# An attention on one Trainium2 core: softmax sums taken by the exponentials, a loop written out, and adds in another order

## The chip, the cores and the metric

The kernel runs on one core of a Trainium2 chip. The metric is the time of one execution on the device in microseconds, lower is better.

## The reference, cut to what is computed

The program is four transformer layers on x of 8 sequences by 100 tokens by 512 features, with a second input `ctx` of 8 by 361 by 512. Each layer adds a cross-attention to `ctx` and a feed-forward block, both behind a layer norm:

```python
x = x + _L0_xattn_ref(_layernorm(x), ctx, ids, ...)
x = x + _L0_ffn_ref(_layernorm(x), ...)
x = x + _L1_xattn_ref(_layernorm(x), ctx, mask, ...)
x = x + _L1_ffn_ref(_layernorm(x), ...)
x = x + _L2_xattn_ref(_layernorm(x), ctx, ...)
x = x + _L2_ffn_ref(_layernorm(x), ...)
x = x + _L3_xattn_ref(_layernorm(x), ctx, ctx, mask, ...)
x = x + _L3_ffn_ref(_layernorm(x), ...)
```

Layer 2's attention, the one whose arithmetic the change touches (16 heads of 32):

```python
Q, K, V = query @ Wq.T + bq, key_value @ Wk.T + bk, key_value @ Wv.T + bv
scores = einsum('bhsd,bhtd->bhst', Q, K) / sqrt(32)
ctx = einsum('bhst,bhtd->bhsd', softmax(scores, axis=-1), V)
return ctx @ Wo.T + bo
```

Layer 1's is the same with the scores clipped to [-50, 50], a mask and a norm on its result. Layer 0's has its keys and values behind a latent, a window of ids as its mask, and 16 heads of 128, so that its output is a product with a weight of 2048 by 512: `out @ W_o`, which is added to x.

## The kernel before

Each engine (PE, ACT, DVE, POOL, and SP for transfers) has its own stream of instructions; they are ordered among each other by semaphores alone. `engine.wait_ge(s, n)` (or `wait`, L94, which leaves out a wait for nothing) holds that engine and all that is queued behind it there. x stays on the chip, features in the partitions, in four blocks of 128 by 800 tokens. Every large product is made of three: values are split into a high and a low part, and `product` (L101) issues high by high (L106), low operand by high (L107) and high by low (L109).

**The two attentions of one class.** `Attention` (layer 2, l2x) and its subclass `BoundedAttention` (layer 1, l1x) go over the 8 sequences, here called contexts. `batches` (L1647) sets how: context 0 in full, contexts 1 to 4 as a loop of two turns with two contexts each, contexts 5 to 7 in full. All five engines' streams are made by it. A context has 4 units m of 4 heads each; unit number i is 4 b + m. In one step PE's queue is (`pe_batch`):

- S, the scores of the next unit (L2158, three products of 4 heads, into the banks 0 to 3). It waits for k_lo of that unit.
- O, the output of the unit before (`pe_output`, L2141): twelve matmuls with a matrix of ones, which put the sum of a row's exponentials into 32 partitions for each head (bank 6), and twelve with the values v.
- the keys of the next context for block m (L106, L107, L109).
- T, twelve transposes of the unit's exponentials (L2124), into the columns 0:400 of the banks 4 to 6. They wait for the exponentials and for `o`, since O's results lie in the same banks, columns 400:500.
- V, the values of the next context (not in step 3).

ACT's queue in a step (`act_batch`): the four exponentials of the next unit (L2165; they wait for DVE's shift), xn_hi of the output (L2203, waits for `o`), k_hi (L1863), at m = 2 the queries of the next context, the copy of T's first two tiles (`turned_01`, L2196), and at m = 1 the high part of the context after next (L1817), for which POOL makes the low part (L1809). DVE's queue (`dve_batch`): maxima of the next unit in two pairs (L2208), each followed by the shift made from it (L2212), the reciprocal of the sums (L2247, 128x100 out of PSUM) and the multiplication with it (L2252, `o`), k_lo (L1869), the copy of T's third tile (`turned_2`, L2235), xn_lo (L2257), and the add of the values' bias (L1875).

**Layer 0's output loop** (l0x) goes over 8 pairs of heads, j; turns 0, 1, 6 and 7 are written out, 2 to 5 are a loop. Before the last turn PE makes in each the fused weight of the next pair (`pe_fuse_output`, 1.4 us), and then four units of twelve products, unit m into the bank pair m % 2; unit m waits for the add of unit m - 2, which frees the banks. ACT takes the high part of the fused weight (L3650) and of the heads' output (L3589), and of three slabs of weights that SP loads (L3645), of which POOL makes the low parts (L3270). DVE makes the low part of the fused weight (L3861), two low parts of the output (L3866) and the four adds into x (L3756), in that order.

## Time and profile before

| | |
|---|---|
| time, median of 3 runs | 2216.07 us (2214.10 to 2216.55) |
| time of the profiled execution | 2215.22 us |
| its span | 2213.3 us |
| busy: PE, DVE, ACT, POOL | 92%, 48%, 41%, 23% |
| mean granted clock of PE | 0.969 |
| layer 0's attention, its feed-forward block | 0 to 497, to 694 us |
| layer 1's | to 965, to 1085 us |
| layer 2's | to about 1385, to 1610 us |
| layer 3's | to 1890, to 2213 us |

Times in the profile are microseconds from the start of the span. PE is the engine of matmuls, PEld its loading of weights, L12 is line 12 of the kernel. In a row of a timeline the square bracket tells how long the engine stood before the instruction and which instruction ended that; "issue" is time in which it waited for nothing that the profile shows. A row may join several like instructions (x4).

### The profile page before, as it was taken

The numbers are of one execution on the slowest core, as the hardware profiler recorded it, in microseconds if no ns is written. First come the engines' busy times: TensorE is split into PE (matmuls) and PEld (weight loads), VectorE is DVE, ScalarE is ACT, GpSimd is POOL, SyncE is SP. The second block draws the span as 40 slices with busy tenths as digits, with TensorE's granted clock in tenths as the row PEclk, the third lists the DMA queues.
The fourth block names the chain that finished last, engine by engine and source line by source line (L and its number), as shares of the span: only waits on it lengthen the run. The fifth ranks groups of instructions, "written<-read, shape, count | busy, mean of one in ns | idle before, by whom it ended". The sixth has DMA issues, their size and how long they took to land.

```text
span 2213.3 us, 39269 instructions
## 1 busy us (share of the span) xinstructions
PE 2034.3 (92%) x14719; PEld 1645.7 (74%) x14719; DVE 1061.3 (48%) x2393; ACT 908.1 (41%) x1740; POOL 501.4 (23%) x358
## 2 busy tenths in 40 slices
PE   7989999887997999977899999999989999799996
PEld 6977776775446877764687777999989999655554
DVE  5556666663114465688646666323244555311111
ACT  3346666432224454576645454422253222222221
POOL 3333332312343211000221010233241110023232
PEclk9999999998998999988999999999999999899998
DMA  3200000228444211131110000222220000589995
GB/s 121 85 14 28 27 28 20 67 99 292 77 84 140 76 67 67 40 153 42 47 47 15 28 14 2 82 63 61 66 75 24 28 27 1 190 281 324 318 323 141
DMA packets 91367, 203.91 MB, mean 92 GB/s; under 512 B 9194, under 2 KB 14414, under 8 KB 89070
## 3 DMA queue, kind: packets, MB, share of 16 engines
q1 hardware_dynamic: 79790, 175.06, 23.8%
q0 software_dynamic: 11424, 26.75, 5.8%
q8 instruction: 104, 1.70, 0.3%
q14 instruction: 49, 0.40, 0.1%
HBM read 184.08 MB, written 21.43 MB: 93 GB/s over the span
## 4 chain that ended last, share of the span: by engine, by line
PE 68%; DMA 12%; DVE 9%; ACT 5%; issue 4%; SPq 1%; POOL 1%; DVEq 0%; ACTq 0%; POOLq 0%
PE psum L106 15%; PE psum L109 14%; PE psum L107 14%; DMA l3f_sum_dram<-l3f_y,l3f_rows 9%; PE psum L900 3%; PE psum L3516 3%; PE psum L3484 2%; PE psum L2710 2%; PE psum L3502 2%; PE psum L2124 2%; PE psum L926 1%; PE psum L2353 1%; PE psum L2725 1%; DVE l2x_highest L2208 1%; PE psum L2938 1%
## 5 line engine op out<-in xcount | busy, mean ns | idle before, releaser
L1534 PE MATMUL psum<-l3f_gate_up,l3f_x_turned 128*128 128x352 f32 x496 | 154.0, 464 | 0.8 <-ACT l3f_x_turned L1593 0.8
L1534 PEld LDWEIGHTS psum<-l3f_gate_up,l3f_x_turned 128*128 128x128 f32 x496 | 92.9, 192 | 48.0 <-issue 1.7
L2165 ACT ACTIVATE l2x_probs<-psum,l2x_shift 100x361 f32<-100x361 f32 x128 | 64.9, 559 | 99.7 <-DVE l2x_shift L2212 98.3
L1809 POOL TENSOR_TENSOR l2x_ctx_lo<-l2x_ctx_raw,l2x_ctx_hi 128x1448 fp32r<-128x1448 f32 x8 | 26.3, 3294 | 330.5 <-ACT l2x_ctx_hi L1817 330.5
L3655 ACT ACTIVATE l0x_probs<-l0x_probs,l0x_lowest 100x361 f32<-100x361 f32 x128 | 75.2, 588 | 42.3 <-DVE l0x_lowest L3819 42.2
L106 PE MATMUL psum<-xn_hi,l2f_w_gu_hi 128*128 128x400 f32 x256 | 88.6, 346 | 1.6 <-DVE xn_lo L192 1.3
L1509 POOL DMA_INDIRECT l3f_sum_dram<-l3f_y,l3f_rows x31 | 49.2, 1586 | 180.3 <-DMA l3f_sum_dram<-l3f_y,l3f_rows 151.7
L1619 DVE TENSOR_TENSOR l3f_h<-l3f_silu,psum 128x352 f32<-128x352 f32 x31 | 16.2, 521 | 151.7 <-ACT l3f_silu L1606 138.3
L107 PE MATMUL psum<-xn_lo,l2f_w_gu_hi 128*128 128x400 f32 x256 | 87.9, 343 | 0.0
L1560 PE MATMUL psum<-l3f_down,l3f_h_turned 128*128 128x512 f32 x186 | 85.1, 593 | 0.9 <-DVE l3f_h_turned L1625 0.9
L2382 ACT ACTIVATE ln_squares<-l1x_clipped,l1x_key_shift,l1x_key_scale 128x400 f32<-128x400 f32 (+1 forms) x96 | 62.3, 712 | 53.3 <-DVE l1x_clipped L2421 53.3
L448 POOL TENSOR_TENSOR l2f_w_gu_lo<-l2f_raw_gu,l2f_w_gu_hi 128x512 fp32r<-128x512 f32 x32 | 43.0, 1356 | 180.9 <-ACT l2f_w_gu_hi L463 180.9
L3819 DVE CUSTOM_DVE_ANT_0 l0x_probs<-psum,l0x_outside 100x361 f32<-100x361 f32 x128 | 62.9, 531 | 32.4 <-PE psum L3484 29.5
L900 PE MATMUL psum<-l0f_weights,l0f_x_turned 128*128 x160 | 74.0, 606 | 1.2 <-ACT l0f_x_turned L1042 0.8
L3516 PE MATMUL psum<-ln_squares,l0x_l_turned 128*128 128x400 f32 (+1 forms) x192 | 73.0, 516 | 0.0
L647 DVE TENSOR_TENSOR l2f_h<-l2f_silu,psum 128x800 f32<-128x800 f32 x16 | 15.8, 988 | 119.1 <-PE psum L109 119.1
L2744 ACT ACTIVATE ln_squares<-psum 64x64 f32<-64x64 f32 x128 | 27.9, 218 | 105.9 <-PE psum L2710 103.5
L1606 ACT ACTIVATE l3f_silu<-psum 128x352 f32<-128x352 f32 x31 | 14.4, 464 | 138.2 <-PE psum L1534 138.2
L109 PE MATMUL psum<-xn_hi,l2f_w_gu_lo 128*128 128x400 f32 x256 | 68.6, 344 | 0.0
L1809 POOL TENSOR_TENSOR l1x_ctx_lo<-l1x_ctx_raw,l1x_ctx_hi 128x1448 fp32r<-128x1448 f32 x8 | 26.5, 3310 | 139.7 <-ACT l1x_ctx_hi L1817 139.7
L2208 DVE TENSOR_REDUCE l2x_highest<-psum 100x2 f32<-100x722 f32 x64 | 57.9, 905 | 0.1
L139 PE MATMUL psum<-identity,residual 128*100 128x128 f32 x248 | 42.0, 340 | 16.5 <-DVE xn_lo L192 5.8
(534 smaller groups left out, 6108.0 us busy)
## 6 DMA issues: line engine op xcount, KB each, us to landing
l3f_gate_up<-in_slabs_dram SPq DMA_DIRECT2D x31, 1280.0 KB, 7.7
l3f_down<-in_slabs_dram SPq DMA_DIRECT2D x31, 512.0 KB
l0x_w_raw<-in_slabs_dram SPq DMA_DIRECT2D x52, 256.0 KB, 2.7
l0f_weights<-in_slabs_dram SPq DMA_DIRECT2D x8, 1536.0 KB
l1x_piece<-in_bit_w_dram SPq DMA_DIRECT2D x8, 1024.0 KB, 6.8
l1f_raw<-in_bit_w_dram SPq DMA_DIRECT2D x8, 1024.0 KB, 9.1
l2f_raw_gu<-in_slabs_dram SPq DMA_DIRECT2D x32, 256.0 KB, 2.6
l3f_down<-in_slabs_dram SPq DMA_DIRECT2D x31, 192.0 KB
```

Of the source, the lines that this page charges most:

```text
L106: pe.matmul(outs[i], weight_hi, moving[i][0], start=first, stop=False)
L107: pe.matmul(outs[i], weight_hi, moving[i][1], start=False, stop=False)
L109: mm = pe.matmul(outs[i], weight_lo, moving[i][0], start=False, stop=last)
L900: mm = pe.matmul(c.psum[:, t % 2, :], self.x_turned[:, t % 2, k, :], self.weights[:, bass.DynSlice(expert, 1), k * 512:(k + 1) * 512].rear ...
L1534: mm = pe.matmul(c.psum[:, bank + x, 0:self.INNER], self.x_turned[:, t % 2, k, :], self.gate_up[:, q, at:at + self.INNER], start=k == 0, s ...
L1560: mm = pe.matmul(c.psum[:, 6 + t % 2, :], self.h_turned[0:z - a, t % 2, k, :], self.down[0:z - a, q, k, :], start=k == 0, stop=k == 2)
L2165: act.activation(self.probs[:, m % 2, g, :], c.psum[0:S, g, 0:C], ACT.Exp, bias=self.shift[:, g:g + 1], scale=self.SCALE).then_inc(self.s( ...
L2208: dve.tensor_reduce(self.highest[:, heads], c.psum[0:S, heads, 0:C], AX.X, ALU.max).then_inc(self.s("maxima"), 1)
L2382: act.activation(self.exps(c, m)[0:z - a, t, :], self.clipped[0:z - a, t, :], ACT.Exp, bias=shift, scale=scale).then_inc(self.s("exps"), 1)
L3516: mm = pe.matmul(c.psum[:, 6, 0:4 * S], self.l_turned[0:z - a, q, t, :], turned[0:z - a, t, :], start=t == 0, stop=t == 2)
L3655: act.activation(self.probs[:, g, :], self.probs[:, g, :], ACT.Exp, bias=self.lowest[:, g:g + 1], scale=-1.0, accum_out=self.total[:, g:g ...
L3819: dve.tensor_tensor_reduce(self.probs[:, g, :], c.psum[0:S, g, 0:C], self.outside[:, q, :], -self.SCALE, 3.0e38, ALU.add, ALU.min, self.lo ...
```

## The change

Three parts.

1. In `Attention`, and so in layer 2 alone: the exponentials also give their sums (`accum_out`, one number for each row and head). DVE turns them into inverses (100x4) and copies each into 32 columns (`by_row`, 100x128); PE transposes that to 128x100 in bank 6, columns 400:500; DVE copies it into SBUF (`spread`), and the multiplication reads it there. The twelve ones-matmuls of each unit and the reciprocal of 128x100 are gone. The transpose stands at the head of PE's step, ahead of the scores, and waits for `by_row` and for `turned_2` of the unit before, whose source lies in the same bank. `BoundedAttention` has methods of its own for its sums; those are not touched.
2. In `BoundedAttention`, layer 1, `batches` writes all 8 contexts out, on all engines; there is no loop.
3. In layer 0's output loop DVE's order is L3861, add 0, low output 0, add 1, low output 1, adds 2 and 3.

```diff
@@ -1644,8 +1644,12 @@
 KEY_TILES = [(0, P), (P, 2 * P), (2 * P, C)]
 
 
-def batches(engine, body):
-
+def batches(engine, body, in_full=False):
+
+    if in_full:
+        for b in range(B):
+            body(b, b % 2, b + 1 < B, b + 2 < B)
+        return
     turns = (B - 4) // 2
     body(0, 0, True, True)
     with engine.Fori(0, turns) as i:
@@ -1666,6 +1670,7 @@
     VALUES_BANK = 7
     EARLY_UNITS = (7,)
     V_SHAPE = [P, 2, 3, D]
+    IN_FULL = False
     SCALE = 1.0 / float(HD) ** 0.5
 
     def __init__(self, name, index, slabs_at):
@@ -1698,7 +1703,9 @@
         self.probs = c.sb(own, n + "_probs", [S, 2, GROUP, C])
         self.highest = c.sb(own, n + "_highest", [S, GROUP])
         self.shift = c.sb(own, n + "_shift", [S, GROUP])
-        self.inverse = c.sb(own, n + "_inverse", [P, S])
+        self.total, self.inverse = (c.sb(own, n + x, [S, 2, GROUP]) for x in ("_total", "_inverse"))
+        self.by_row = c.sb(own, n + "_by_row", [S, 2, P])
+        self.spread = c.sb(own, n + "_spread", [P, S])
         self.o = c.sb(own, n + "_o", [P, 2, S])
 
     def turned(self, c):
...
@@ -1956,6 +1963,7 @@
         self.pe_scores(c, pe, 0, 0, 0)
 
     def pe_after_batches(self, c, pe):
+        self.pe_inverse(c, pe, B * KD - 1, KD - 1)
         self.pe_output(c, pe, B - 1, (B - 1) % 2, KD - 1)
 
     def pe_outputs_ready(self, pe):
...
@@ -2071,6 +2079,7 @@
         self.dve_project(c, dve)
 
     def dve_last_output(self, c, dve):
+        self.dve_spread(c, dve, B * KD - 1)
         self.dve_output(c, dve, B - 1, KD - 1)
         self.dve_output_low(c, dve, B - 1, KD - 1)
 
@@ -2100,6 +2109,8 @@
 
         for m in range(KD):
             i = b * 4 + m
+            if m or not isinstance(b, int) or b:
+                self.pe_inverse(c, pe, i - 1, m + 1)
             if m < 3:
                 self.pe_scores(c, pe, b, q, m + 1)
             elif more:
@@ -2127,6 +2138,13 @@
             if more and m < 3:
                 self.pe_values(pe, b + 1, 1 - q, m)
 
+    def pe_inverse(self, c, pe, i, m):
+
+        pe.wait_ge(self.s("by_row"), i + 1)
+        pe.wait_ge(self.s("turned_2"), i + 1)
+        pe.transpose(c.psum[:, 6, 400:400 + S], self.by_row[:, m % 2, :], c.identity[0:S, 0:S]).then_inc(
+            self.s("inverse_units"), 1)
+
     def pe_output(self, c, pe, b, q, m):
 
         i, turned = b * 4 + m, self.turned(c)
@@ -2134,15 +2152,11 @@
         pe.wait_ge(self.s("turned_2"), i + 1)
         if m == 0:
             pe.wait_ge(self.s("v_added"), b * 3 + 3)
-        for x in range(2):
-            for t, (a, z) in enumerate(KEY_TILES):
-                for g in range(GROUP):
-                    head = slice((m * GROUP + g) * HD, (m * GROUP + g + 1) * HD)
-                    mm = pe.matmul(c.psum[g * HD:(g + 1) * HD, 4 + m % 2 if x else 6, 400:400 + S],
-                                   self.v[0:z - a, q, t, head] if x else c.ones[0:z - a, 0:HD],
-                                   turned[0:z - a, t, g * S:(g + 1) * S], start=t == 0, stop=t == 2)
-            if x == 0:
-                mm.then_inc(self.s("total_units"), 1)
+        for t, (a, z) in enumerate(KEY_TILES):
+            for g in range(GROUP):
+                head = slice((m * GROUP + g) * HD, (m * GROUP + g + 1) * HD)
+                mm = pe.matmul(c.psum[g * HD:(g + 1) * HD, 4 + m % 2, 400:400 + S], self.v[0:z - a, q, t, head],
+                               turned[0:z - a, t, g * S:(g + 1) * S], start=t == 0, stop=t == 2)
         mm.then_inc(self.s("pv_units"), 1)
 
     def pe_scores(self, c, pe, b, q, m):
@@ -2163,7 +2177,7 @@
         wait(act, self.s("t_units"), i - 1)
         for g in heads:
             act.activation(self.probs[:, m % 2, g, :], c.psum[0:S, g, 0:C], ACT.Exp, bias=self.shift[:, g:g + 1],
-                           scale=self.SCALE).then_inc(self.s("exps"), 1)
+                           scale=self.SCALE, accum_out=self.total[:, m % 2, g:g + 1]).then_inc(self.s("exps"), 1)
 
     def act_before_batches(self, c, act):
         self.act_exps(c, act, 0, 0, range(0, 2))
@@ -2173,7 +2187,17 @@
         self.dve_maxima(c, dve, 0, 0)
         self.dve_maxima(c, dve, 0, 1)
         self.dve_values(dve, 0, 0, 1)
+        self.dve_inverse(dve, 0, 0)
         self.dve_values(dve, 0, 0, 2)
+
+    def dve_inverse(self, dve, i, m):
+        dve.wait_ge(self.s("exps"), (i + 1) * GROUP)
+        dve.reciprocal(self.inverse[:, m % 2, :], self.total[:, m % 2, :]).then_inc(self.s("inverses"), 1)
+        dve.wait_ge(self.s("inverses"), i + 1)
+        wait(dve, self.s("inverse_units"), i - 1)
+        dve.tensor_copy(self.by_row[:, m % 2, :].rearrange("p (g e) -> p g e", g=GROUP),
+                        self.inverse[:, m % 2, :].unsqueeze(2).broadcast_to([S, GROUP, HD])).then_inc(
+                            self.s("by_row"), 1)
 
     def act_batch(self, c, act, b, q, more, two_more):
         turned = self.turned(c)
@@ -2216,6 +2240,8 @@
         turned = self.turned(c)
         for m in range(KD):
             i = b * 4 + m
+            if m or not isinstance(b, int) or b:
+                self.dve_spread(c, dve, i - 1)
             if m < 3 or more:
                 self.dve_maxima(c, dve, i + 1, 0)
                 self.dve_maxima(c, dve, i + 1, 1)
@@ -2237,19 +2263,23 @@
                 self.dve_output_low(c, dve, b, m - 1)
             elif not isinstance(b, int) or b:
                 self.dve_output_low(c, dve, b - 1, KD - 1)
+            if m < 3 or more:
+                self.dve_inverse(dve, i + 1, m + 1)
             if more and m < 3:
                 self.dve_values(dve, b + 1, 1 - q, m)
 
+    def dve_spread(self, c, dve, i):
+        dve.wait_ge(self.s("inverse_units"), i + 1)
+        wait(dve, self.s("o"), i)
+        dve.tensor_copy(self.spread[:, :], c.psum[:, 6, 400:400 + S]).then_inc(self.s("spread"), 1)
+
     def dve_output(self, c, dve, b, m):
         i = b * 4 + m
-        dve.wait_ge(self.s("total_units"), i + 1)
-        wait(dve, self.s("o"), i)
-        dve.reciprocal(self.inverse[:, :], c.psum[:, 6, 400:400 + S]).then_inc(self.s("inverses"), 1)
-        dve.wait_ge(self.s("inverses"), i + 1)
+        dve.wait_ge(self.s("spread"), i + 1)
         dve.wait_ge(self.s("pv_units"), i + 1)
         wait(dve, self.s("o_hi"), i - 1)
         wait(dve, self.s("o_lo"), i - 1)
-        dve.tensor_tensor(self.o[:, m % 2, :], c.psum[:, 4 + m % 2, 400:400 + S], self.inverse[:, :], ALU.mult).then_inc(
+        dve.tensor_tensor(self.o[:, m % 2, :], c.psum[:, 4 + m % 2, 400:400 + S], self.spread[:, :], ALU.mult).then_inc(
             self.s("o"), 1)
 
     def dve_output_low(self, c, dve, b, m):
@@ -2264,6 +2294,7 @@
 
 class BoundedAttention(Attention):
     BOUND = 50.0
+    IN_FULL = True
     EPS = 1e-8
     SCALE_MAX = 0.3
 
@@ -3738,23 +3769,24 @@
         self.dve_normalise(c, dve, 0)
         batches(dve, lambda b, q, more, two_more: self.dve_batch(c, dve, b, q, more))
 
-        def split_output(j, q):
-            self.low_fused(c, dve, j, q)
-            for x in range(2):
-                self.low_output(c, dve, j, q, x)
+        def added(j, m):
+            dve.wait_ge(self.s("out_units"), j * 4 + m + 1)
+            if not isinstance(j, int) or j:
+                dve.wait_ge(self.s("added"), j * 4 + m - 3)
+            into = c.residual[:, m, :].rearrange("p (h t) -> p h t", h=2)
+            dve.tensor_tensor(into, into, c.psum[:, 2 * (m % 2):2 * (m % 2) + 2, 0:HALF], ALU.add).then_inc(
+                self.s("added"), 1)
 
         def out(j, q, more):
-            if more:
-                split_output(j + 1, 1 - q)
             if not more:
                 return tail_dve(dve, c.norms[self.index + 1], last_added)
-            for m in range(KD):
-                dve.wait_ge(self.s("out_units"), j * 4 + m + 1)
-                if not isinstance(j, int) or j:
-                    dve.wait_ge(self.s("added"), j * 4 + m - 3)
-                into = c.residual[:, m, :].rearrange("p (h t) -> p h t", h=2)
-                dve.tensor_tensor(into, into, c.psum[:, 2 * (m % 2):2 * (m % 2) + 2, 0:HALF], ALU.add).then_inc(
-                    self.s("added"), 1)
+            self.low_fused(c, dve, j + 1, 1 - q)
+            added(j, 0)
+            self.low_output(c, dve, j + 1, 1 - q, 0)
+            added(j, 1)
+            self.low_output(c, dve, j + 1, 1 - q, 1)
+            added(j, 2)
+            added(j, 3)
 
         def last_added(h, m):
             j, u = self.PAIRS - 1, h * KD + m
```

The hunks left out pass `self.IN_FULL` to `batches` in the other engines' streams.

## Rows read from the trace of the kernel before

**Rows 1.** Busy us by stretch (windows): layer 2's attention; columns PE, PEld, DVE, ACT, POOL.
```profile
1137.00:1385.00 248.00, 231.09 (x2912) 187.84 (x2911) 157.74 (x310) 125.11 (x234) 24.89 (x10) 1.00 0.06 18
```

**Rows 2.** Waits of the stretch 391 to 497 us: total, times, longest.
```profile
PE psum L106 <- DVE residual L3756: 9.7, 8, 1.3
```

**Rows 3.** Timeline of layer 0's output loop: start, duration, engine, line.
```profile
408.18 1.02 ACT L3650 ACTIVATE l0x_out_w_hi<-psum 128x1024 fp32r<-128x1024 f32 x1 [7.81 <-PE psum L109]
...
410.37 2.44 DVE L3866 TENSOR_TENSOR l0x_o_lo<-l0x_q_latent,l0x_o_hi 128x800 fp32r<-128x800 f32 x2
...
412.73 1.87 DVE L3756 TENSOR_TENSOR residual<-residual,psum 128x800 f32<-128x800 f32 x2
...
413.76 0.45 PE L106 MATMUL psum<-l0x_o_hi,l0x_out_w_hi 128*128 128x400 f32 x1 [1.33 <-DVE residual L3756]
...
419.83 1.03 ACT L3650 ACTIVATE l0x_out_w_hi<-psum 128x1024 fp32r<-128x1024 f32 x1 [7.76 <-PE psum L109]
```

**Rows 4.** Busy us by stretch (windows): two contexts of layer 1; PEclk stands near the end.
```profile
777.30:805.40 28.10, 26.90 (x424) 22.32 (x428) 18.01 (x40) 14.74 (x25) 3.33 (x1) 1.00 0.21 65
805.40:838.60 33.20, 28.48 (x426) 23.66 (x428) 18.09 (x41) 14.38 (x24) 3.32 (x1) 0.95 0.16 57
```

**Rows 5.** Timeline of PE at layer 1's back edge.
```profile
830.69 0.43 PE L106 MATMUL psum<-l1x_ctx_hi,l1x_w_hi 128*128 128x362 f32 x1 [4.33 <-issue]
```

**Rows 6.** Waits of the stretch 1137 to 1385 us, the longest of kind issue.
```profile
PEld psum L2124 <- issue: 4.7, 9, 1.3
```

**Rows 7.** Timeline of one step of layer 2's attention.
```profile
1240.43 0.42 PE L2158 MATMUL psum<-l2x_k_hi,l2x_qh_hi 32*100 32x362 f32 x4
...
1241.11 0.72 PE L2141 MATMUL psum<-ln_squares,ones 128*32 128x100 f32 x24
...
1241.65 0.70 PE L2141 MATMUL psum<-ln_squares,l2x_v 128*32 128x100 f32 x24
...
1242.48 2.12 ACT L2165 ACTIVATE l2x_probs<-psum,l2x_shift 100x361 f32<-100x361 f32 x4 [4.17 <-DVE l2x_shift L2212]
...
1243.48 0.78 DVE L2247 RECIPROCAL l2x_inverse<-psum 128x100 f32<-128x100 f32 x1
...
1245.09 1.27 PE L2124 MATMUL psum<-identity,l2x_probs 100*128 100x100 f32 x12 [0.55 <-DVE l2x_o L2252]
1245.16 0.55 ACT L1863 ACTIVATE l2x_k_hi<-psum,l2x_vectors 128x362 fp32r<-128x362 f32 x1
1245.74 0.59 DVE L1869 SCALAR_TENSOR_TENSOR l2x_k_lo<-psum,l2x_vectors,l2x_k_hi 128x362 fp32r<-128x362 f32 x1 [0.90 <-ACT l2x_k_hi L1863]
...
1249.37 0.41 PE L2158 MATMUL psum<-l2x_k_hi,l2x_qh_hi 32*100 32x362 f32 x4
```

**Rows 8.** Timeline at the turn of a context in layer 2.
```profile
1258.63 0.41 PE L2158 MATMUL psum<-l2x_k_hi,l2x_qh_hi 32*100 32x362 f32 x4
...
1263.66 0.59 DVE L1869 SCALAR_TENSOR_TENSOR l2x_k_lo<-psum,l2x_vectors,l2x_k_hi 128x362 fp32r<-128x362 f32 x1 [0.90 <-ACT l2x_k_hi L1863]
...
1264.21 0.41 PE L2158 MATMUL psum<-l2x_k_hi,l2x_qh_hi 32*100 32x362 f32 x4
...
1264.32 0.58 DVE L2235 COPY ln_squares<-psum 105x400 f32<-105x400 f32 x1
```

**Rows 9.** Timelines of layer 2: POOL's splits of two contexts, and DVE beside the first.
```profile
1248.61 3.31 POOL L1809 TENSOR_TENSOR l2x_ctx_lo<-l2x_ctx_raw,l2x_ctx_hi 128x1448 fp32r<-128x1448 f32 x1 [29.36 <-ACT l2x_ctx_hi L1817]
1281.00 3.29 POOL L1809 TENSOR_TENSOR l2x_ctx_lo<-l2x_ctx_raw,l2x_ctx_hi 128x1448 fp32r<-128x1448 f32 x1 [29.09 <-ACT l2x_ctx_hi L1817]
...
1251.21 0.73 DVE L2212 TENSOR_SCALAR l2x_shift<-l2x_highest 100x2 f32<-100x2 f32 x1
```

**Rows 10.** Timeline of ACT in layer 0: exponentials with accumulation.
```profile
216.19 0.60 ACT L3655 ACTIVATE l0x_probs<-l0x_probs,l0x_lowest 100x361 f32<-100x361 f32 x1 [1.05 <-DVE l0x_lowest L3819]
216.69 0.19 ACT L3655 ACTIVATION_READ_ACCUMULATOR l0x_probs<-l0x_probs,l0x_lowest 100x1 f32 x1
216.78 0.58 ACT L3655 ACTIVATE l0x_probs<-l0x_probs,l0x_lowest 100x361 f32<-100x361 f32 x1
```

More of the change, by code:

```diff
@@ L1765, in body @@
                     self.slab(c, sp, i)
-        batches(sp, body)
+        batches(sp, body, self.IN_FULL)
     def sync_more(self, c, sp):
@@ L1799, in body @@
                     self.split_weight(pool, i)
-        batches(pool, body)
+        batches(pool, body, self.IN_FULL)
     def split_output_weights(self, act, b, m):
@@ L1915, in pe @@
         self.pe_start(c, pe)
-        batches(pe, lambda b, q, more, two_more: self.pe_batch(c, pe, b, q, more))
+        batches(pe, lambda b, q, more, two_more: self.pe_batch(c, pe, b, q, more), self.IN_FULL)
         self.pe_after_batches(c, pe)
@@ L2023, in act @@
         self.act_before_batches(c, act)
-        batches(act, lambda b, q, more, two_more: self.act_batch(c, act, b, q, more, two_more))
+        batches(act, lambda b, q, more, two_more: self.act_batch(c, act, b, q, more, two_more), self.IN_FULL)
         self.act_finish(c, act)
@@ L2061, in dve @@
         self.dve_before_batches(c, dve)
-        batches(dve, lambda b, q, more, two_more: self.dve_batch(c, dve, b, q, more))
+        batches(dve, lambda b, q, more, two_more: self.dve_batch(c, dve, b, q, more), self.IN_FULL)
         self.dve_finish(c, dve)
```

## The prediction, made before the changed kernel was run

> **What bounds the kernel now.** The busy windows come first: in layer 2's attention PE is busy 231 of 248 us at the full clock [rows 1]. That speaks for less work on PE, but PE waits in most steps too, so each stretch is read from its waits and its timeline.
>
> Layer 0's output loop: among the waits PE stands 9.7 us, in 8 places, for an add of L3756 [rows 2]. In the timeline of an iteration (11.65 us, from one L3650 to the next) DVE has its queue in this order: L3861, two L3866 (2.44 us), then the add that frees the bank, ending 0.93 us after its start at 412.73. PE's third unit waits for it 1.33 us, to 413.76 [rows 3].
>
> Layer 1: one context takes 28.1 us, the one that holds the loop's back edge 33.2 [rows 4]. There PE stands 4.33 us, for nothing that the profile shows ("issue") [rows 5].
>
> Layer 2: the longest such wait is 1.3 us [rows 6], so no back edge costs anything like that. The timeline of a step [rows 7] shows a ring. S (scores) at 1240.43; DVE takes maxima; ACT starts four exponentials at S+2.05 (2.12 us); then k_hi and DVE's k_lo, to 1246.33; PE's values V start 0.06 later and the next S follows them. PE is not the ring's slow part: it runs out of work before T (transposes), where it waits 0.55 us for o (L2252), and V stands behind T's 1.27 us in PE's queue. At the turn of a context there is no V: S starts at 1264.21, right at the end of T, 5.58 us after the S before [rows 8].
>
> **Layer 0's adds.** No instruction is new; add 0 goes ahead of both L3866 and add 1 between them. Add 0 then follows L3861's end at 410.46 and ends about 411.45; PE wants it at 412.3. L3866, add 1: 412.7, 413.7, and PE wants that one at 414.5. The second L3866 and adds 2 and 3 end at about 417.7, still before the next fused product's L3861 needs DVE. PE's wait goes: four units of 12 products at 0.18 us (8.8) and the fusion's 6 (1.4) leave 10.15 us an iteration, 1.5 less; seven iterations give -10.5. What is late next is ACT's L3650, which waits for PE alone, then POOL's split and SP's slabs, whose slack of over 1 us in the period stays. Bounds: -7 (1 us each) to -11.
>
> **Layer 1 in full.** Same instructions, on all five engines (SP's context loads and POOL's split too), no branch. The stall's price is 33.2 less 28.1: -5.1. Bounds: 0, if it is code that comes late however it is laid out, and -5.1.
>
> **Layer 2.** Removed on PE: 12 ones-matmuls a unit, 0.54 us between the first of the ones group and the first of the values group [rows 7]; added: one transpose, 0.1 us (a twelfth of T's 1.27). Over 32 units that is -14 us of PE work. On DVE the reciprocal of 0.78 us goes; a reciprocal and a copy of 100 rows (0.17 us each, as L2212 [rows 9], the nearest of that size) and the spread (a quarter us, as the multiplication of L2252) come. Both removals lie between S and T, where PE stands for exponentials and o anyhow. So I follow the ring:
> - S to first exponential. DVE's v-add (0.69 us) ends at S+0.79, and the maxima follow at once; the spread now goes between them: 2.05+0.24.
> - Exponentials. An accumulating one is followed by a read of 0.19 us, and the next starts 0.09 us after that read [rows 10]: 0.59 apart instead of 0.52, and 0.1 behind the last. I take +0.31 a unit. From below it is 0; from above 0.75, four whole reads.
> - First exponential to k_hi: 2.68 in the row, held by o; o is now early, and 2.12+0.31 with xn_hi's 0.2 and gaps is 2.70. k_hi to the end of k_lo 1.17, to V 0.06, V to S 2.98, and the new transpose ahead of S 0.10.
> The sum is 9.30 instead of 8.94 us. The steps that were longer than that already (9.26, where DVE's shift took 0.73 us beside POOL's split [rows 9]) gain nothing and lose nothing: 9.30.
> - The turn. The new transpose waits for turned_2 of the unit before and stands ahead of S on PE. turned_2 (0.58 us, L2235) is queued on DVE behind k_lo. S+2.29+2.70+1.17 gives k_lo's end at 6.16, turned_2 at 6.79, transpose, S at 6.96, where it was 5.58. Behind it wait S, the maxima and all the ring.
> A context went 32.4 us (from the two splits [rows 9]); it goes 9.30x3+6.96 = 34.86, +2.4. Seven contexts with a successor: +16.8. The last output loses reciprocal and ones (1.3) from the tail and pays slower exponentials (0.4): -0.9. Together +16. Bounds: with reads and spread at nothing only the turn's share and the transpose are left, +8; with serial reads (0.44 more a unit, 14) some +25 after what other waits cover.
>
> **Sum.** -10.5-5.1+16 = +0.4. On the profiled execution's 2215.22 us that is 2215.6; the median of the three runs lies 0.85 above that execution, so **2216.5**. A change under 0.2%, 4.4 us, is about what a measurement of this kernel can't tell from none.
>
> **The pages.** The Trainium skill, "Runtime: NRT & Kernel Launch", section "Instruction fetch mechanics", says that a taken branch to a target outside the current two pages of instructions forces a fetch before execution goes on. Layer 1's stall agrees with that; layer 2's loop, where no row shows one, doesn't. By the page the whole 5.1 us go, and a DVE or ACT loop that grows could get such a stall of its own.
>
> **Rivals.**
> 1. PE's work counts (0.08). PE is busy 93% of the stretch [rows 1], and if the o wait (0.55) and the ones are what sets the step, layer 2 gives -14, and the whole is 2215.2-10.5-5.1-14+0.85 = 2186.5. Against it: S to T is filled by exponentials in the row; V waits for k_lo.
> 2. Cheap accumulation (0.20). The reads overlap and the spread slips in: layer 2 +8, 2208.5. For it: ACT's reads overlap the next exponential by half already [rows 10].
> 3. **Slower**: DVE's new small copy, by_row, meets POOL's split of 3.31 us (0.25). The shift of 0.17 us took 0.73 there [rows 9]. In the new step by_row comes 7.3 to 7.5 us after S (turned_2's end at 6.8, output_low 0.25, reciprocal 0.17), and POOL's split at 7.8, where the rows have 8.2: T needs no o any more and ends half a microsecond earlier [rows 7, 9]. They miss each other by 0.3 us. If it falls in and is held by about 1.7 us, six splits give +10: 2226.5. It decides when ACT's L1817 ends earlier than by_row starts. Serial reads (+9) end in the same place. For a held copy speaks the Trainium skill, "SBUF — State Buffer", section "SBUF: two separate sides": VectorE and GpSimd share a pair of ports as an exclusive lock. The row of L2212 agrees with it in part: it waited about 0.56 us, not for all of the split.
> 4. Layer 1's stall stays, or moves into another stretch (0.07): 2221.6.
> 5. PE's clock: the context with the 4.33 us of standing shows a mean granted clock of 0.95 of the full 2.4 GHz, where the one before shows 1.00 [rows 4]; a turn with some 1.9 us of standing in place of 0.3 might do so too. After the 1.33 us in the output loop it did not [rows 3]. I give this no chance of its own; its price, some tenths of a microsecond per turn, is inside the upper bound.
> That a part does nothing at all (DVE's order hidden in layer 0) would need that PE waits there for another; the waits name only the add [rows 2].
>
> **How the numbers follow.** Forecast 0.40, at 2216.5, its own range 2212 to 2221. Rivals 1 and 2 are faster, 0.28, and a little of the forecast's own lower side: faster 0.31. Rivals 3 and 4 are slower, 0.32, less what of them stays within 4.4 us: slower 0.29. Same 0.40. The range leaves out rival 1 and the ends of rivals 2 and 3: 2204 to 2227.
>
> **What would show it.** Layer 0: iteration of 10.15 us, no wait for L3756 on PE. Layer 1: all splits of contexts 28.1 us apart. Layer 2: PE's new transpose waits for L2235 about 1.3 us at each turn; V steps at 9.3; splits 34.9 apart; reads of about 0.19 us behind each L2165. The forecast is wrong if the splits there stay near 32 us apart (rival 2, or 1 below that), or if by_row's copy takes over half a microsecond (rival 3).

## The result, and where the time went

The changed kernel takes 2203.3 us (median of 5 runs, 2202.33 to 2206.84); the kernel before took 2216.55 on the same chip (5 runs). The ratio is 0.9944, with a 95% interval from 0.9930 to 0.9959. It is faster by some 12 us. The forecast was no change, at 2216.5, and the measured time lies just under its range of 2204 to 2227.

The page of the changed kernel (first part):

```profile
span 2201.5 us, 37754 instructions
...
PE 2013.6 (91%) x13983; PEld 1630.8 (74%) x13983; DVE 1047.7 (48%) x2457; ACT 911.4 (41%) x1868; POOL 504.4 (23%) x358
```

PE has 736 matmuls fewer and is busy for 20.7 us less, yet its share of the span fell only from 92% to 91%. Lined up with the trace before, by the start of like instructions on POOL and ACT, the time moves thus:

| stretch | forecast | profiled executions |
|---|---|---|
| layer 0's output loop | -10.5 | -10.4 |
| layer 0's feed-forward block | 0 | +2.3 |
| layer 1's attention | -5.1 | -6.1 |
| layer 2's attention | +16 | +3.1 |
| everything else | 0 | -0.7 |
| span | +0.4 | -11.8 |

The +3.1 us of layer 2 is too low by 1.7 us: the profiled execution of the kernel before had a stretch of low clock (0.53, 1384.00 to 1387.50) behind its last scores. From there to the feed-forward block it took 30.9 us, where e1, e2, e4 and e6, in which this code is as before, took 29.2; the changed kernel took 27.2.

**Layer 0.** The timeline of ACT in the output loop, the rows that answer to [rows 3] (L3681 was L3650):

```profile
396.55 1.02 ACT L3681 ACTIVATE l0x_out_w_hi<-psum 128x1024 fp32r<-128x1024 f32 x1 [1.83 <-PE psum L109]
...
416.69 1.03 ACT L3681 ACTIVATE l0x_out_w_hi<-psum 128x1024 fp32r<-128x1024 f32 x1 [6.16 <-PE psum L109]
...
457.21 1.02 ACT L3681 ACTIVATE l0x_out_w_hi<-psum 128x1024 fp32r<-128x1024 f32 x1 [6.29 <-PE psum L109]
```

From 396.55 to 457.21 are six iterations, 10.11 us each, where the forecast had 10.15 and the kernel before 11.65. Of the eight waits of PE for an add one is left, 1.2 us in the last turn.

**Layer 1.** The timeline of POOL, the split of each context (L1816 was L1809):

```profile
774.52 3.32 POOL L1816 TENSOR_TENSOR l1x_ctx_lo<-l1x_ctx_raw,l1x_ctx_hi 128x1448 fp32r<-128x1448 f32 x1 [8.16 <-ACT l1x_ctx_hi L1824]
802.45 3.31 POOL L1816 TENSOR_TENSOR l1x_ctx_lo<-l1x_ctx_raw,l1x_ctx_hi 128x1448 fp32r<-128x1448 f32 x1 [24.61 <-ACT l1x_ctx_hi L1824]
830.34 3.32 POOL L1816 TENSOR_TENSOR l1x_ctx_lo<-l1x_ctx_raw,l1x_ctx_hi 128x1448 fp32r<-128x1448 f32 x1 [24.58 <-ACT l1x_ctx_hi L1824]
```

They are 27.93 and 27.89 us apart. The context with the stall ([rows 4], 33.2 us) is like the others, and all of them are 0.2 us shorter than the 28.1 of before.

**Layer 2.** The waits of PE, 1120 to 1376 us (total, times, longest):

```profile
PE psum L106 <- DVE l2x_k_lo L1876: 15.9, 21, 1.2
PE psum L2145 <- DVE ln_squares L2261: 12.5, 11, 1.4
PE psum L2135 <- ACT l2x_probs L2179: 1.7, 3, 0.8
```

Two of them are new or nearly so: V waits for k_lo in all 21 steps that have values (before, 1.4 us in 3 of them), and the new transpose (L2145) waits 12.5 us for turned_2 (L2261). Now one step with values, to set beside [rows 7]. New lines: L2172 scores, L1882 v-add, L2274 spread, L2232 maxima, L2179 exponentials, L2227 xn_hi, L1870 k_hi, L1876 k_lo:

```profile
1237.21 0.41 PE L2172 MATMUL psum<-l2x_k_hi,l2x_qh_hi 32*100 32x362 f32 x4
1237.23 0.69 DVE L1882 TENSOR_TENSOR l2x_v<-psum,l2x_bv 128x512 f32<-128x512 f32 x1 [2.14 <-PE psum L109]
...
1237.84 0.25 DVE L2274 COPY l2x_spread<-psum 128x100 f32<-128x100 f32 x1
...
1238.01 0.91 DVE L2232 TENSOR_REDUCE l2x_highest<-psum 100x2 f32<-100x722 f32 x1
...
1239.24 0.56 ACT L2179 ACTIVATE l2x_probs<-psum,l2x_shift 100x361 f32<-100x361 f32 x1 [3.65 <-DVE l2x_shift L2236]
...
1239.70 0.19 ACT L2179 ACTIVATION_READ_ACCUMULATOR l2x_probs<-psum,l2x_shift 100x1 f32 x1
1239.80 0.55 ACT L2179 ACTIVATE l2x_probs<-psum,l2x_shift 100x361 f32<-100x361 f32 x1
...
1241.44 0.28 ACT L2227 ACTIVATE xn_hi<-l2x_o 128x100 f32 x1
1241.61 0.56 ACT L1870 ACTIVATE l2x_k_hi<-psum,l2x_vectors 128x362 fp32r<-128x362 f32 x1
...
1242.21 0.59 DVE L1876 SCALAR_TENSOR_TENSOR l2x_k_lo<-psum,l2x_vectors,l2x_k_hi 128x362 fp32r<-128x362 f32 x1 [1.60 <-ACT l2x_k_hi L1870]
...
1242.86 0.48 PE L106 MATMUL psum<-l2x_w_hi,l2x_ctx_hi 128*105 128x512 f32 x1 [0.73 <-DVE l2x_k_lo L1876]
...
1245.95 0.42 PE L2172 MATMUL psum<-l2x_k_hi,l2x_qh_hi 32*100 32x362 f32 x4
```

S to S is 8.74 us; the forecast had 9.30, the row before 8.94. Two prices of the forecast are not paid here.

The first is the spread, which takes 0.17 us from its start to that of the maxima. The v-add starts 0.02 us after S, where before it was 0.10, since the transpose now stands between V and S: that makes 0.08 us of room. The rest was there before. The maxima wait for the scores as well as for the v-add; in the trace of the kernel before they start at S+0.80 at the turns too (1265.01, with S at 1264.21), where no v-add stands ahead of them. So they still start at S+0.80, and the exponentials at S+2.03.

The second is the reads of the sums. First exponential to xn_hi is 2.20 us (1239.24 to 1241.44), and the kernel before had 2.21 in the loop where `o` held it least (1251.97 to 1254.18 in its trace). But there ACT stood twice within that time, for the second shift and 0.09 us for `o`. The reads now fill these stands; what they cost where there are none, e4 shows.

The turn of a context, to set beside [rows 8]:

```profile
1250.95 0.59 DVE L1876 SCALAR_TENSOR_TENSOR l2x_k_lo<-psum,l2x_vectors,l2x_k_hi 128x362 fp32r<-128x362 f32 x1 [1.60 <-ACT l2x_k_hi L1870]
1251.46 0.56 DVE L2261 COPY ln_squares<-psum 105x400 f32<-105x400 f32 x1
...
1252.17 0.28 PE L2145 MATMUL psum<-identity,l2x_by_row 100*128 100x100 f32 x1 [1.30 <-DVE ln_squares L2261]
...
1252.38 0.55 PE L2172 MATMUL psum<-l2x_k_hi,l2x_qh_hi 32*100 32x362 f32 x4
...
1252.72 0.52 PE L2172 MATMUL psum<-l2x_k_lo,l2x_qh_hi 32*100 32x362 f32 x4
...
1253.58 0.91 DVE L2232 TENSOR_REDUCE l2x_highest<-psum 100x2 f32<-100x722 f32 x1 [0.74 <-PE psum L2172]
...
1254.84 0.56 ACT L2179 ACTIVATE l2x_probs<-psum,l2x_shift 100x361 f32<-100x361 f32 x1 [3.09 <-DVE l2x_shift L2236]
```

The mechanism is the forecast's: turned_2 behind k_lo, then the transpose, then S, at 6.43 us after the S before (1245.95) in place of 5.58; the forecast had 6.96. What the forecast gave no chance of its own came too: after the stand of 1.30 us the scores' products take 0.52 us instead of 0.33. The granted clock beside it, for the three microseconds after this turn and after another with the same stand:

```profile
1252.30:1255.30 3.00, 3.00 (x39) 2.18 (x39) 2.07 (x5) 0.47 (x2) 0.00 (x0) 0.53 0.00 0
1219.70:1222.70 3.00, 3.00 (x47) 2.54 (x47) 2.32 (x5) 0.89 (x3) 0.00 (x0) 1.00 0.00 0
```

The number behind the five engines' is the granted clock: 0.53 here, near the lower of the two levels, and 1.00 at the other turn. It fell behind two of the seven turns, in e5's trace behind the same two. Here it cost 0.7 us (the step after this turn is 9.43 instead of 8.72). Behind the last turn, where PE goes from the scores to T without a stand, it cost 1.5 us: the step is 7.35 instead of 5.83. One product in that step, one in the next, and the clock (0.50) of the first:

```profile
1351.53 0.54 PE L107 MATMUL psum<-xn_lo,l2x_w_hi 128*128 128x400 f32 x1
...
1358.88 0.35 PE L107 MATMUL psum<-xn_lo,l2x_w_hi 128*128 128x400 f32 x1
...
1351.50:1354.50 3.00, 3.00 (x10) 2.98 (x10) 1.52 (x5) 2.46 (x9) 0.00 (x0) 0.50 0.01 3
```

Between the scores of units 1 and 31 the four traces of kernels with the transpose ahead of the scores (changed, e3, e5, e11) have two or three such falls each. The ten others, in which the scores of a turn start without a stand, have none. That ties the falls to this order, but not each to its turn: one in e3 (at 1160.11) and one in e11 (at 1159.15) began in a step with values, and cost 1.6 and 1.7 us.

### The profile page after: what moved, and what is told of

It reads as the page before. It is cut to its first block, busy times and chain, and to the rows that moved or that the text cites. A ratio compares the mean times of both kernels' runs of the same rounds, so it can differ in the third digit from the quotient of the medians.

```text
span 2201.5 us, 37754 instructions
## 1 busy us (share of the span) xinstructions
PE 2013.6 (91%) x13983; PEld 1630.8 (74%) x13983; DVE 1047.7 (48%) x2457; ACT 911.4 (41%) x1868; POOL 504.4 (23%) x358
## 4 chain that ended last, share of the span: by engine, by line
PE 66%; DMA 12%; DVE 9%; ACT 7%; issue 4%; SPq 1%; POOL 1%; DVEq 0%; ACTq 0%; POOLq 0%
PE psum L106 15%; PE psum L109 14%; PE psum L107 14%; DMA l3f_sum_dram<-l3f_y,l3f_rows 9%; PE psum L900 3%; PE psum L3547 3%; PE psum L3515 2%; PE psum L2741 2%; ACT l2x_probs L2179 2%; PE psum L3533 2%; PE psum L926 1%; PE psum L2384 1%; PE psum L2756 1%; PE psum L2969 1%; DVE l2x_highest L2232 1%
## 5 line engine op out<-in xcount | busy, mean ns | idle before, releaser
L2179 ACT ACTIVATE l2x_probs<-psum,l2x_shift 100x361 f32<-100x361 f32 x128 | 70.4, 559 | 122.0 <-DVE l2x_shift L2236 122.0
L1816 POOL TENSOR_TENSOR l2x_ctx_lo<-l2x_ctx_raw,l2x_ctx_hi 128x1448 fp32r<-128x1448 f32 x8 | 26.4, 3300 | 332.1 <-ACT l2x_ctx_hi L1824 332.1
L106 PE MATMUL psum<-xn_hi,l2f_w_gu_hi 128*128 128x400 f32 x256 | 88.6, 346 | 1.6 <-DVE xn_lo L192 1.3
L2775 ACT ACTIVATE ln_squares<-psum 64x64 f32<-64x64 f32 x128 | 27.9, 218 | 105.8 <-PE psum L2741 103.4
L2232 DVE TENSOR_REDUCE l2x_highest<-psum 100x2 f32<-100x722 f32 x64 | 57.9, 905 | 3.4 <-PE psum L2172 3.1
L1816 POOL TENSOR_TENSOR l1x_ctx_lo<-l1x_ctx_raw,l1x_ctx_hi 128x1448 fp32r<-128x1448 f32 x8 | 26.4, 3306 | 134.7 <-ACT l1x_ctx_hi L1824 134.7
L1816 POOL TENSOR_TENSOR l3x_ctx_lo<-l3x_ctx_raw,l3x_ctx_hi 128x1448 fp32r<-128x1448 f32 x8 | 26.3, 3289 | 131.9 <-ACT l3x_ctx_hi L1824 131.9
```

What stands on the lines that cost most here:

```text
L106: pe.matmul(outs[i], weight_hi, moving[i][0], start=first, stop=False)
L1816: pool.tensor_tensor(self.ctx_lo[:, q, :, :], self.ctx_raw[:, :, :], self.ctx_hi[:, q, :, :], ALU.subtract).then_inc(self.s("ctx_split"), 1)
L2179: act.activation(self.probs[:, m % 2, g, :], c.psum[0:S, g, 0:C], ACT.Exp, bias=self.shift[:, g:g + 1], scale=self.SCALE, accum_out=self.t ...
L2232: dve.tensor_reduce(self.highest[:, heads], c.psum[0:S, heads, 0:C], AX.X, ALU.max).then_inc(self.s("maxima"), 1)
```

## Experiments

Each was measured in turn with the kernel before on its chip; e1 to e4, e5 to e8 and e9 to e12 had one chip each, so between these groups ratios are compared. "Layer 2" is the time from the scores of unit 1 to those of unit 31 in the trace, 235.6 us in the kernel before.

| run | median us | ratio to before | 95% interval | layer 2, us |
|---|---|---|---|---|
| changed kernel | 2203.30 | 0.9944 | 0.9930 to 0.9959 | 242.3 |
| e1, adds only | 2207.00 | 0.9955 | 0.9940 to 0.9970 | |
| e2, layer 1 only | 2212.70 | 0.9978 | 0.9967 to 0.9989 | |
| e3, layer 2 only | 2222.70 | 1.0028 | 1.0017 to 1.0039 | 243.6 |
| e4, sums alone | 2217.67 | 1.0003 | 0.9993 to 1.0012 | 236.3 |
| e5, changed again | 2206.19 | 0.9953 | 0.9940 to 0.9966 | 242.4 |
| e6, without layer 2's part | 2200.06 | 0.9922 | 0.9909 to 0.9935 | 235.0 |
| e7, transpose behind the scores | 2196.90 | 0.9914 | 0.9902 to 0.9927 | 231.9 |
| e8, e7 and layer 2 written out | 2191.93 | 0.9892 | 0.9878 to 0.9906 | 228.6 |
| e9, old sums, layers 1 and 2 written out | 2195.52 | 0.9904 | 0.9883 to 0.9924 | 231.0 |
| e10, e8 with ones for nothing | 2199.02 | 0.9919 | 0.9899 to 0.9939 | 233.4 |
| e11, changed, spread twice | 2208.74 | 0.9962 | 0.9949 to 0.9975 | 247.0 |
| e12, e8, low part and inverses later | 2191.49 | 0.9887 | 0.9865 to 0.9909 | 225.8 |

**e1: which part does what, the adds.** Its edit is the last hunk of the diff alone.

> The kernel before with layer 0's adds moved, nothing else. Theory: PE's wait for the add was the whole of the loss, so an iteration of the output loop takes 10.1 us instead of 11.65 and the loop's end comes 10.4 us earlier; in the trace of the changed kernel 2.3 us of that were gone again at the end of the feed-forward block behind it (its last product waits for transfers of rows by index). If that loss belongs to the earlier start, this run is 8 us faster, about 2208.4, ratio 0.9963. Rival: the 2.3 us were chance of that one execution, and the run is 10.4 us faster, 2206.1, ratio 0.9953.

Measured 0.9955, some 10 us; the interval (6.7 to 13.3 us) holds both 8 and 10.4, so the time doesn't tell them apart. The traces do. From the last product of the output loop to the last of the feed-forward block, in which PE waits for rows that POOL moves by index, the fourteen traces of this study have between 200.2 and 204.2 us. Both ends are kernels whose layer 0 is as before (the kernel before and e4); the ten with the adds moved have 200.4 to 202.1, and the 202.1 is the changed kernel's. Its +2.3 us is within what these transfers differ by from one execution to the next. The theory as I had put it falls; the adds are worth their 10 us.

**e2: layer 1.**

```diff
 class BoundedAttention(Attention):
     BOUND = 50.0
+    IN_FULL = True
```

> The kernel before with layer 1's contexts written out, nothing else. Theory: the stall of 4.33 us at the back edge and the slow clock behind it go (5.1 us), and each of the four contexts that were in the loop runs 0.2 us shorter (27.9 instead of 28.1 in the trace of the changed kernel): 6.0 us faster, 2210.5, ratio 0.9973. Rival: the stall was not the loop's, and comes up elsewhere: ratio 1.000.

0.9978 is 4.9 us, with 2.4 to 7.3 in the interval, and from the second to the last of its eight splits the trace is 6.1 us shorter (173.8 instead of 179.9). The stall was the loop's.

**e3: layer 2 alone.** All of the first part of the change; layer 1 has its loop again, and the adds are as before.

> The kernel before with the new sums of layer 2, nothing else. Theory, by the trace of the changed kernel: steps with values 8.7 us where they were 8.7 to 9.2, turns 6.43 where they were 5.58, and slower steps without keys; +3.4 us in all, 2220, ratio 1.0015. The forecast's +16 would be 2232.5, ratio 1.0072. Rival: removed matmuls and reciprocal do pay here, and the loss in the changed kernel came with the other parts: ratio 0.999 or below.

It is slower by 6.2 us (3.8 to 8.6): the sign of the forecast and less than half of its size. This trace also shows the third rival at work, though not where the forecast saw it. In context 0 POOL splits weights (L1784), and DVE's small instructions from SBUF to SBUF run into it, by_row as well as the shift. The same pair in the changed kernel, POOL first, then DVE; and the two rows that the rival was about, where by_row passes the context's split by 0.6 us:

```profile
1139.49 1.29 POOL L1784 TENSOR_TENSOR l2x_w_lo<-l2x_out_raw,l2x_w_hi 128x512 fp32r<-128x512 f32 x1
1145.50 1.30 POOL L1784 TENSOR_TENSOR l2x_w_lo<-l2x_out_raw,l2x_w_hi 128x512 fp32r<-128x512 f32 x1 [4.72 <-ACT l2x_w_hi L1789]
...
1139.64 1.16 DVE L2236 TENSOR_SCALAR l2x_shift<-l2x_highest 100x2 f32<-100x2 f32 x1
...
1145.63 1.24 DVE L2198 COPY l2x_by_row<-l2x_inverse 100x128 f32<-100x128 f32 x1
...
1234.87 0.23 DVE L2198 COPY l2x_by_row<-l2x_inverse 100x128 f32<-100x128 f32 x1
...
1235.68 3.30 POOL L1816 TENSOR_TENSOR l2x_ctx_lo<-l2x_ctx_raw,l2x_ctx_hi 128x1448 fp32r<-128x1448 f32 x1 [29.25 <-ACT l2x_ctx_hi L1824]
```

The shift, 0.17 us elsewhere, ends at 1140.80 and POOL at 1140.78; by_row, 0.23 us elsewhere, at 1146.87 and POOL at 1146.80. Each is held to POOL's end. So was the shift of [rows 9] (1251.94, with POOL's end at 1251.92), which the prediction read as held "in part": it had only started late. The rule of the Trainium skill, "SBUF — State Buffer", section "SBUF: two separate sides", that the loser of the shared pair is blocked for the whole instruction of the other, agrees with all three. One more thing follows in every context: T ends earlier, the high part of the context too, and POOL's split begins before the next shift and is over at 1238.98, just ahead of it at 1239.04. The steps that were 9.2 us for that reason are 8.7.

The two held instructions cost little. The exponentials behind the held shift start at S+2.94, where before, with the shift held too, it was S+2.71; behind the held by_row DVE stands 0.62 us for the next values anyhow. The stretch of 243.6 us in e3's own trace holds three falls of the clock, one more than the changed kernel's 242.3.

**e4: what the reads cost.**

```diff
+        self.sums = c.sb(own, n + "_sums", [S, 2, GROUP])
...
-                           scale=self.SCALE).then_inc(self.s("exps"), 1)
+                           scale=self.SCALE, accum_out=self.sums[:, m % 2, g:g + 1]).then_inc(self.s("exps"), 1)
```

> The kernel before, its layer 2 unchanged except that the exponentials also write their sums, which nothing reads; ones-matmuls and reciprocal stay. Theory: the read of the sum runs beside the next instruction of ACT, four exponentials and the one behind them take what they took, and steps stay as they are: ratio 1.000, within 1 us. The forecast's price of 0.31 us a unit: +10 us, ratio 1.0045. Whole serial reads of 0.19 us: +24 us, ratio 1.011.

1.0003: 128 reads of 0.2 us cost under 3 us (the interval), and 0.7 in layer 2's stretch. The loop's steps and turns are those of before (5.58 and 8.7 to 9.2). In the contexts written out they are not: steps of 8.33 to 8.38 us became 8.50 to 8.54. Timeline of ACT in such a step, the kernel before and then e4:

```profile
1329.94 2.02 ACT L2165 ACTIVATE l2x_probs<-psum,l2x_shift 100x361 f32<-100x361 f32 x4 [0.99 <-DVE l2x_shift L2212]
1331.94 0.29 ACT L2203 ACTIVATE xn_hi<-l2x_o 128x100 fp32r<-128x100 f32 x1
...
1330.20 0.56 ACT L2166 ACTIVATE l2x_probs<-psum,l2x_shift 100x361 f32<-100x361 f32 x1 [4.14 <-DVE l2x_shift L2213]
...
1332.36 0.30 ACT L2204 ACTIVATE xn_hi<-l2x_o 128x100 fp32r<-128x100 f32 x1
```

First exponential to xn_hi is 2.16 us with the reads and 2.00 without: 0.16 a unit, half of the forecast's 0.31, and in the loop, where ACT stood that long anyhow, nothing. The second exponential of a unit starts 0.46 us after the first without a read and 0.55 with it, though each is recorded with 0.56.

**e6: without layer 2's part.** e5 is the changed kernel again, for the comparison.

> The changed kernel once more, on the chip of the next three, so that they can be set against it. By the three parts alone (0.9955, 0.9978, 1.0028) it is 0.9961; by its first measurement 0.9944.

> Layer 0's adds and layer 1 in full, layer 2 as before. Theory: layer 2's part costs 3.4 to 6 us in the changed kernel, so leaving it out gives ratio 0.9930 to 0.9935 to before, about 15 us, and 3 to 6 us under the changed kernel. Rival: the parts are not additive, layer 2's part is free once the others are in, and this equals the changed kernel.

6.1 us less than the changed kernel by the medians. So the parts add up: the change would be 6 us better without its largest part. The traces have 5.3 us for it, from the scores of unit 0 to the feed-forward block (270.7 and 276.0 in e5).

**e7: the transpose behind the scores.**

```diff
-            if m or not isinstance(b, int) or b:
-                self.pe_inverse(c, pe, i - 1, m + 1)
             if m < 3:
                 self.pe_scores(c, pe, b, q, m + 1)
             elif more:
                 self.pe_scores(c, pe, b + 1, 1 - q, 0)
+            if m or not isinstance(b, int) or b:
+                self.pe_inverse(c, pe, i - 1, m + 1)
```

and `dve_spread` likewise behind the two `dve_maxima`.

> The changed kernel with the transpose of the inverses behind the scores on PE and the spread behind the maxima on DVE. Theory: at each turn the scores start with k_lo, at S+5.7 instead of S+6.43, but DVE's turned_2, xn_lo, inverse and by_row then end at S+6.6 and hold the maxima, so the exponentials come 0.6 us earlier and not 0.8; the stand of 1.3 us on PE before the transpose goes, and with it the slow clock behind two turns (some 1.2 us); in steps with values the 0.17 us of the transpose leave the ring: 8.55 instead of 8.72. Together 7 x 0.6 + 1.2 + 21 x 0.17 = 9 us less than the changed kernel. Rival: the wait only changes its place, from the scores to the output behind them, and nothing is gained: equal to the changed kernel.

9.3 us less than e5, as the theory had it in sum, but not from where it said. Its turn:

```profile
1214.67 0.41 PE L2172 MATMUL psum<-l2x_k_hi,l2x_qh_hi 32*100 32x362 f32 x4
...
1215.13 0.56 DVE L2261 COPY ln_squares<-psum 105x400 f32<-105x400 f32 x1
...
1215.85 0.28 PE L2145 MATMUL psum<-identity,l2x_by_row 100*128 100x100 f32 x1 [0.43 <-DVE ln_squares L2261]
...
1216.57 0.91 DVE L2232 TENSOR_REDUCE l2x_highest<-psum 100x2 f32<-100x722 f32 x1 [0.35 <-issue]
...
1217.82 0.56 ACT L2179 ACTIVATE l2x_probs<-psum,l2x_shift 100x361 f32<-100x361 f32 x1 [2.21 <-DVE l2x_shift L2236]
```

S starts at 5.04 us after the S before (1209.63), right at T's end: sooner than the 5.7 expected, because the k_lo of this step belongs to a later unit, and this S never waits for it. The transpose stands only 0.43 us, and no step is slowed by the clock. But now DVE holds the maxima (S+1.90), as expected, and the exponentials start at S+3.15 here and at S+2.7 in most turns. The exponentials' delay makes the step after a turn 9.2 to 9.7 us long, where it was 8.6 to 9.4. Of the loop's two other steps with values one got 0.07 to 0.09 us shorter, not 0.17, since the maxima came only that much nearer to V; in the other one the exponentials now start at S+2.09 to 2.18 instead of 2.03, and nothing is gained. The gain is in the turns: the loop's contexts are 31.9 to 32.1 us apart, where the changed kernel has 32.6 to 33.3.

**e8 and e9: written out, with new and with old sums.** e8 is e7 with `IN_FULL = True` for layer 2, e9 is e6 with it.

> As e7, and layer 2's contexts written out too. Theory: in full code the exponentials start 1.94 to 1.95 us after the scores instead of 2.05, so 16 steps of the loop save 0.1 us each, 1.8 us under e7. Rival: a larger code stalls somewhere as layer 1's loop did, and it is slower than e7 by some 5 us.

> e6 (the other two parts, layer 2's sums as before) with layer 2 written out. Against e8 it has the same loops and differs in the sums alone. Theory: writing out gives e6 some 3 us by its shorter steps, ratio 0.991; e8 with its 0.9892 stays 4 us better, so the new sums do pay once the transpose is out of the way. Rival: what e8 won it won by writing out, and this equals e8.

Writing out gives 4 to 5 us, more than the 1.8 and 3 expected; the traces show 3.3 and 4.0 in layer 2 (by time the intervals overlap in both pairs). The best reading of the new sums is e8 against e9: 2.4 us in layer 2's stretch of the traces. By time it is 0.9892 against 0.9904, with intervals that overlap, so that the new sums pay at all is shown by the traces only.

The steps tell where. In a middle context e8's turn is 4.83 us and e9's 5.35, but the step after it is 9.3 and not 8.7, and the next 8.5 and not 8.4. What is left is the third step, 8.6 instead of 9.05: with the old sums POOL's split holds the shift there (exponentials at S+2.67), with the new ones it hardly does (S+2.0). Behind the last scores e8 gains 1.3 us more (27.9 instead of 29.2 up to the feed-forward block).

**e10: does work on PE count?** Ahead of the output in `pe_output`, into the same bank:

```diff
-        for t, (a, z) in enumerate(KEY_TILES):
-            for g in range(GROUP):
+        for x in range(2):
+            for t, (a, z) in enumerate(KEY_TILES):
+                for g in range(GROUP):
...
+                                   self.v[0:z - a, q, t, head] if x else c.ones[0:z - a, 0:HD],
```

> e8 with the twelve ones-matmuls of each unit put back on PE, into the bank of the output ahead of it, where the output then overwrites them: the same results, 0.54 us more of PE a unit. Theory: in the steps with values PE stands 0.7 us for k_lo, and takes them for nothing; they cost at the seven turns and in the last context's four units, where PE is what ends last: 11 x 0.54 = 6 us over e8, ratio about 0.992. Rival, PE is the bound everywhere: 32 x 0.54 = 17 us over e8, ratio 0.997.

Timeline of PE in a step with values (L2174 scores, L2135 T, L106 the first of V; ones, output and keys lie between the first two):

```profile
1200.13 0.41 PE L2174 MATMUL psum<-l2x_k_hi,l2x_qh_hi 32*100 32x362 f32 x4
...
1204.30 1.22 PE L2135 MATMUL psum<-identity,l2x_probs 100*128 100x100 f32 x12
1206.15 0.48 PE L106 MATMUL psum<-l2x_w_hi,l2x_ctx_hi 128*105 128x512 f32 x1 [0.63 <-DVE l2x_k_lo L1876]
```

Ones and all, T starts at S+4.17 instead of e8's 3.66, and V still waits 0.63 us for k_lo. 17.3 us of work cost 4.8 us in layer 2 (228.6 to 233.4), and 6 us by the ratios, whose intervals overlap. The sum is as forecast, but less than half of it comes from where the theory said. The turns go from 4.83 to 5.32, but the step behind each gets back 0.4 of that: 1.4 us together. The last context costs 0.7. About half, 2.3 us, comes by a way that I had not named: T later means POOL's split later, and the shift in the step after it is held again (exponentials at S+2.4 in place of 2.0).

**e11: is there room for the spread?**

```diff
+        dve.tensor_copy(self.spread2[:, :], c.psum[:, 6, 400:400 + S])
         dve.tensor_copy(self.spread[:, :], c.psum[:, 6, 400:400 + S]).then_inc(self.s("spread"), 1)
```

> The changed kernel with the copy of the spread inverses made twice (the second into a buffer that nothing reads). Theory: the first fits between the end of the v-add and the maxima to the last tenth, because the transpose ahead of the scores leaves the scores 0.17 us behind the v-add; a second one has no such room and costs 0.25 us in each of the 20 steps with values, 5 us over the changed kernel, ratio 0.9965 to 0.997. Rival: DVE has slack there and it costs nothing, 0.9944 to 0.9953.

DVE in the gap between v-add and maxima (L1883, twice the spread, L2233):

```profile
1181.49 0.69 DVE L1883 TENSOR_TENSOR l2x_v<-psum,l2x_bv 105x512 f32<-105x512 f32 x1 [1.64 <-PE psum L109]
1182.10 0.25 DVE L2275 COPY l2x_spread<-psum 128x100 f32<-128x100 f32 x1
1182.27 0.25 DVE L2276 COPY l2x_spread<-psum 128x100 f32<-128x100 f32 x1
1182.44 0.90 DVE L2233 TENSOR_REDUCE l2x_highest<-psum 100x2 f32<-100x722 f32 x1
```

Copies are 0.17 us apart, their 0.25 us overlapping, and the second puts the exponentials from S+2.04 to S+2.20 and steps from 8.72 to 8.87; layer 2 is 4.7 us longer. 1.7 of that are one step of 10.96 instead of 9.24 us, in which the clock fell (1159.15) where the changed kernel's did not; the rest is the copy's. The room was for one copy and no more. The times (0.9962 against 0.9953 of e5) agree in sign, and their intervals overlap.

**e12: DVE's queue at the turn.** In e8, at m = 3, `dve_output_low` and `dve_inverse` are left out, and made in the next step behind `dve_output`.

> e8, and at the seven turns DVE makes xn_lo and the inverses behind the next unit's maxima and output, ahead of k_lo, instead of between turned_2 and the maxima. Theory: in the trace of e7 the first exponentials of a context start 2.7 us after the scores where 1.95 is what the maxima need; the 0.75 us go at each turn: 5 us under e8, ratio 0.987. Rival: PE's keys and output, not DVE, hold the step after the turn, and nothing is gained.

The maxima (L2232) now follow turned_2 (L2264):

```profile
1211.81 0.57 DVE L2264 COPY ln_squares<-psum 105x400 f32<-105x400 f32 x1
1212.29 0.90 DVE L2232 TENSOR_REDUCE l2x_highest<-psum 100x2 f32<-100x722 f32 x1
```

The exponentials start at S+2.19 instead of 2.71, contexts are 30.7 us apart instead of 31.2, and layer 2's stretch is 2.8 us shorter: half of what was expected, since turned_2 itself still stands ahead of them. In the time of the whole kernel it can't be seen (0.9887 and 0.9892). e8 and e12 are 24 us faster than the kernel before and some 11 to 14 us faster than the changed one.

## Why the prediction was wrong

- *Layer 0's adds, -10.5 us:* right, 10.4 us in the trace, 10 us by e1, and by the wait that it named.
- *Layer 1 in full, -5.1 us:* right; 4.9 us by e2, 6.1 in the trace. The 0.2 us that each other context also gained was not foreseen.
- *Layer 2, +16 us:* the sign was right, the size was not; it is 6 us by e3 and by e6 against e5, and in the two profiled executions 3, or 5 without the low clock in the one of before. This is what put the result out of the range. The steps that failed are two prices of the sum and one effect that was left out.
  - "the spread now goes between them: 2.05+0.24". It cost nothing. I read the maxima as held by the v-add alone. They wait for the scores too, which left 0.09 us of room, and the transpose ahead of S moved S by another 0.08 against the v-add. e11 shows that the gap holds just one copy.
  - "I take +0.31 a unit" for the reads. The traces have 0.16 a unit in the contexts written out and nothing in the loop, 0.7 us in all by e4's. It was priced from the distance of 0.59 in layer 0's row against 0.52; in layer 2 it is 0.55 with a read, and what it adds fell into stands of ACT.
  - With both out, a context of the sum is 2.3 us shorter (three steps by 0.58 and the turn by 0.53), 16 us for seven, more than layer 2's whole error. What comes back is partly the two slow clocks, 0.7 us and 1.5; the 1.5 is most of the last context's loss, whose steps took 1.9 us more and not 0.4. And the sum took 8.94 us as the step before for every context, where in the contexts written out most steps were 8.1 to 8.7: in context 0 the three steps ahead of the turn took 0.9 us more than before, in context 6 0.4. The tail behind the last scores was 2.0 us shorter (27.2 against the 29.2 of e6), where I had 1.3.
  - "gain nothing and lose nothing" for the steps of 9.26 us: they gained 0.5, since the split no longer meets the shift.
- *"Both removals lie between S and T, where PE stands for exponentials and o anyhow":* right in the main. e10 shows that 17.3 us of matmuls are worth 5 to 6, and half of that by way of POOL's split.
- *The turn:* mechanism right, and it is the part that makes layer 2 slower; e7 takes it away and gets 9 us.
- *The rivals.* The first (PE's work counts, -14) is excluded by e3 and e10. The second (cheap accumulation) is what came true in layer 2, at +8 forecast and 3 to 6 measured, with both bounds of the sum at their lower ends at once. The third happened in context 0 with other instructions of POOL: two instructions held by 1 us each, of which hardly 0.2 us reached the ring. The fourth is excluded by e2. The fifth, without a chance of its own, came behind two turns of seven, at 0.7 and 1.5 us.

What stays open: why the clock fell behind two of seven turns whose stands were alike (1.30 to 1.41 us); and why the contexts of layer 1 are 0.2 us shorter in full, also those that had been written out before.

## What to carry to other kernels

When an instruction is put into two queues at once, price each from the moment at which both have moved: a wait or an instruction ahead of one engine's work gives the other engine room. A new instruction at the head of an in-order queue should be asked what it waits for at the one turn where that comes late; here four lines moved behind the scores were worth as much as a whole part of the change. And matmuls taken from an engine that is busy for 93% of a stretch bought at most a third of their time, because a ring through ACT and DVE sets the step; half of that came from a collision between two other engines that happened to go away.
